# One attention layer of a decoder: a local and a global unit's values back to back, with copies, loads and the residual sum reordered around them

## The reference, cut to what matters

```python
x = x + attn(layernorm(x), ...)      # this layer is what the change touches
x = x + xattn(layernorm(x), ctx_1024, mask, ...)
x = x + ffn(layernorm(x), ...)       # 8 experts, top 2

def attn(x, ...):                    # x is (16, 256, 256): 16 batch rows, 256 tokens, width 256, 16 heads of 16
    x = x + pos_emb[:S]
    w = x.reshape(B, nW, 128, H, hd)                                  # windows of 128 tokens
    local = softmax(w @ w.T * scale) @ w                              # within a window, by head
    comp = conv(x, conv_w, stride 4) + conv_b                         # 64 compressed tokens a row
    gt = concatenate([comp, global_memory])                           # 128 global tokens
    glob = softmax(x @ gt.T * scale) @ gt                             # by head
    mix = sigmoid(concatenate([local, glob]) @ gate_w + gate_b)
    return (mix * local + (1 - mix) * glob) @ out_w + out_b
```

## Time and profile before

| what | value |
|---|---|
| three runs | 1135.87, 1140.89, 1145.44 us; median 1140.89 |
| profiled execution, its own time | 1146.37 us |
| its span, first to last instruction | 1144.5 us |
| granted TensorE clock over the span | 0.983 |
| PE busy | 1073.8 us (94%) |
| DVE, ACT, POOL busy | 675.0 (59%), 647.5 (57%), 543.9 us (48%) |
| self-attention | up to 438 us of the span |
| PE, DVE, ACT busy from 150 to 200 us | 48.11, 42.31, 30.87 of 50 us |

### The profile page before, as it was taken

How to read it: one execution, slowest core, us unless ns; L and a number is a source line. 1 busy time by engine, 2 the same in 40 slices (tenths; PEclk the granted TensorE clock), 3 DMA queues, 4 the chain that set the end, 5 groups by cost and what they waited for, 6 DMA issues and landing times.

```text
span 1144.5 us, 28496 instructions
## 1 busy us (share of the span) xinstructions
PE 1073.8 (94%) x11049; PEld 919.7 (80%) x11049; DVE 675.0 (59%) x1341; ACT 647.5 (57%) x870; POOL 543.9 (48%) x646
## 2 busy tenths in 40 slices
PE   7899999999999987999999998899999999999995
PEld 6777777787777765777777776799999999999995
DVE  4488888889878875788887888322424222222221
ACT  2466666656665653777776765444445444445441
POOL 6534455353653322443665553457654444444442
PEclk9899999999999997999999999999999999999999
DMA  8673653636436332566666567675433322233221
GB/s 214 168 179 109 148 152 88 180 107 160 128 83 183 77 100 48 149 189 174 145 150 150 144 159 205 181 174 56 42 52 49 52 47 48 47 51 51 48 42 24
DMA packets 174563, 130.23 MB, mean 114 GB/s; under 512 B 60810, under 2 KB 162927, under 8 KB 174432
## 3 DMA queue, kind: packets, MB, share of 16 engines
q1 hardware_dynamic: 155280, 106.79, 35.6%
q0 software_dynamic: 15840, 18.77, 11.7%
q10 hardware_dynamic: 3312, 2.85, 0.9%
HBM read 88.29 MB, written 40.08 MB: 112 GB/s over the span
## 4 chain that ended last, share of the span: by engine, by line
PE 48%; DMA 5%; DVE 3%; issue 2%; ACT 1%; another core or an unknown queue 1%; POOL 1%; SPq 1%; POOLq 0%; ACTq 0%
PE ps_scores L1861 22%; PE ps_out L1879 10%; PE ps_turn L1724 3%; DMA weights<-q_scr 3%; PE ps_misc L1756 2%; PE ps_out L1736 2%; PE ps_scores L1711 2%; PE ps_misc L1677 2%; DMA q_scr<-qp 2%; PE ps_turn L1840 1%; PE ps_misc L1744 1%; PE ps_scores L1704 1%; DVE xa_rowmax L2398 1%; DVE ps_scores L2395 1%; PE ps_turn L1766 1%
## 5 line engine op out<-in xcount | busy, mean ns | idle before, releaser
L1861 PEld LDWEIGHTS ps_scores<-xgT,weights 128*128 128x128 f32 x2272 | 263.8, 192 | 5.6 <-ACT xgT L2080 1.7
L1861 PE MATMUL ps_scores<-xgT,weights 128*128 128x128 f32 x2272 | 265.9, 275 | 1.4 <-ACT xgT L2080 1.1
L2367 DVE TENSOR_TENSOR gate<-ps_scores,silu 128x512 f32<-128x512 f32 x71 | 49.1, 692 | 243.7 <-ACT silu L2096 224.1
L915 ACT ACTIVATE weights<-ps_scores 128x1024 f32<-128x1024 f32 x128 | 126.9, 1023 | 81.1 <-PE ps_scores L608 65.7
L2096 ACT ACTIVATE silu<-ps_scores 128x512 f32<-128x512 f32 x71 | 42.4, 597 | 207.7 <-PE ps_scores L1861 199.1
L1879 PE MATMUL ps_out<-w2s,gate 128*128 x560 | 132.8, 380 | 0.8 <-DVE y L2373 0.8
L2089 ACT COPY weights<-weights 128x2048 f32 x68 | 129.9, 1910 | 0.5
L1879 PEld LDWEIGHTS ps_out<-w2s,gate 128*128 128x128 f32 x560 | 100.9, 190 | 12.3 <-issue 1.5
L1081 DVE TENSOR_REDUCE sa_rowmax<-ps_turn 128x8 bf16<-128x1024 f32 x64 | 77.7, 1215 | 34.4 <-PE ps_turn L585 34.4
L920 ACT CAST weights<-ps_scores 8x1024 bf16<-8x1024 f32 x64 | 64.3, 1004 | 54.2 <-PE ps_scores L599 54.2
L1555 POOL DMA_INDIRECT table<-entry,slot_i x64 | 64.7, 1011 | 47.1 <-PE ps_out L1736 24.8
(11 more groups left out here) (294 smaller groups left out, 2100.8 us busy)
## 6 DMA issues: line engine op xcount, KB each, us to landing
weights<-w_scr SPq DMA_DIRECT2D x60, 256.0 KB, 4.2
weights<-q_scr SPq DMA_DIRECT2D x96, 128.0 KB
ks<-w_scr SPq DMA_DIRECT2D x24, 256.0 KB, 3.8
weights<-k_scr SPq DMA_DIRECT2D x48, 120.0 KB
w_scr<-wp SPq DMA_DIRECT2D x7, 768.0 KB, 3.6
q_scr<-qp SPq DMA_DIRECT2D x14, 384.0 KB
weights<-in_w1T SPq DMA_DIRECT2D x10, 512.0 KB
weights<-in_w3T SPq DMA_DIRECT2D x10, 512.0 KB
```

Source lines behind the costliest of these rows:

```text
L915: act.activation(probs[s % 2][:], m.scores[s % 2][:], ACT.Exp, scale=SCALE).then_inc(exped, 1)
L1861: mm = pe.matmul(h_ps[r % 2][:, j, c, :], weights[:, j, k, c * P:(c + 1) * P], xgT[r % 2][:, k, :], start=(k == 0), stop=(k == DT - 1))
```

## The change: what it does, and the diff

Self-attention only. (1) On PE the two `values` calls of units 2k and 2k+1 follow each other, in four places of a row: behind `subtract_max(b+1, 0)`, behind `gate(b-1, 0)` (in odd rows behind `scores(b, 4)`), behind `gate(b-1, 1)` and behind `subtract_max(b, 6)` (in even rows behind `compress`). (2) Local probabilities get a second buffer, `m.first_probs`; an exponential of a local unit waits for the values four units back. `first_exponentials`, which wrote that buffer already, waits until it is read. (3) `turn_max` stands ahead of `scores` in each place, and ACT copies the turned maxima ahead of the context's copy. (4) `turn_c` writes `side[0]` (a half of `m.turn`) and no longer `m.misc`; `queries_scores(b, 3)` waits until ACT has read it. (5) On DVE `residual(b-2)` stands behind `maxima(b, 1)`, `apply_norm(b+3)` behind `maxima(b, 3)`, `mix_row(b-1)` behind `maxima(b, 7)`; in odd rows `maxima(b, 4)` stands ahead of `turn_out(b, 0, 0)`. (6) On SP the loads of a stack don't wait for each other, the store is a step of its own ahead of the last row's keys and values, and `load_g` stands ahead of `load_ctx`.

```diff
-    probs = m.wide
+    local_probs, global_probs = [m.wide[0], m.first_probs], m.wide[1]
+    probs = lambda U: global_probs if U % 2 else local_probs[U // 2 % 2]
...
-                if paced and (s > 2 or under_way):
-                    sp.wait_ge(loaded[s % 3], before + 16 * (s // 3))
+                if paced and under_way and s < 3:
+                    sp.wait_ge(loaded[s], before)
...
-        def stack_w(p):
+        def store_w(p):
             i = p % 2
             sp.wait_ge(w_split, 3 * R * (p + 1))
...
+        def stack_w(p):
+            i = p % 2
             sp.wait_ge(w_stored, 16 * p + 16)
...
+            store_w(p)
+            store_keys_values(R * p - 1)
             stack_w(p)
             store_g(p)
-            store_keys_values(R * p - 1)
+            load_g(p)
             load_ctx(R * p + 1)
-            load_g(p)
...
+            if old:
+                values(b - 1, UPR - 2)
+                values(b - 1, UPR - 1)
+            if not some:
+                first_scores()
+
+            if some:
+                turn_max(b, 1)
+                scores(b, 2)
             if more:
+                turn_c(b + 1, side[0])
+            if nxt or last and even:
                 if old:
                     pe.wait_ge(proj_read, b - 1)
...
-                turn_c(b + 1, m.misc)
-            if old:
-                values(b - 1, UPR - 1)
-            if some:
-                scores(b, 2)
-                turn_max(b, 1)
-            if nxt or last and even:
-                pe.wait_ge(cT_read, b + 2)
...
             if some:
-                values(b, 0)
                 keys_scores(b, 1)
             if some:
+                if more:
+                    pe.wait_ge(cT_read, b + 2)
                 queries_scores(b, 3)
                 subtract_max(b, 2)
...
                 gate(b - 1, 0)
-            if some:
+            if some and even:
+                values(b, 0)
                 values(b, 1)
             if some:
+                turn_max(b, 3)
                 scores(b, 4)
-                turn_max(b, 3)
+            if some and not even:
+                values(b, 0)
+                values(b, 1)
...
-                values(b, 2)
                 keys_scores(b, 3)
...
                 gate(b - 1, 1)
             if some:
+                values(b, 2)
                 values(b, 3)
             if some:
+                turn_max(b, 5)
                 scores(b, 6)
-                turn_max(b, 5)
...
-                values(b, 4)
                 keys_scores(b, 5)
...
                 if nxt and even:
                     compress(p + 1, 1)
+                values(b, 4)
                 values(b, 5)
+            if some:
+                turn_max(b, 7)
             if more:
                 scores(b + 1, 0)
-            if some:
-                turn_max(b, 7)
...
-                values(b, 6)
                 keys_scores(b, 7)
...
-            if U > 1:
+            if s % 2 and U > 1:
                 act.wait_ge(valued, U - 1)
-            act.activation(probs[s % 2][:], m.scores[s % 2][:], ACT.Exp, scale=SCALE).then_inc(exped, 1)
+            elif U > 3:
+                act.wait_ge(valued, U - 3)
+            act.activation(probs(U)[:], m.scores[s % 2][:], ACT.Exp, scale=SCALE).then_inc(exped, 1)
...
             act.wait_ge(m.shifted, 1)
+            act.wait_ge(valued, UPR * NB - 1)
...
                 exponentials(b, 0)
+            if some:
+                copy_max(b, 1)
             if more:
-                copy_cT(b + 1, m.misc)
-            if some:
-                copy_max(b, 1)
+                copy_cT(b + 1, side[0])
...
                 maxima(b, 1)
+            if b > 1:
+                residual(b - 2)
             if old:
                 turn_out(b - 1, 1, 1)
...
                 divide(b - 1, 1, 1)
+            if not some:
+                first_maxima()
+            if some:
+                maxima(b, 3)
             if ahead:
                 apply_norm(b + 3)
-            if not some:
-                first_maxima()
-            if some:
-                maxima(b, 3)
-                turn_out(b, 0, 0)
-                maxima(b, 4)
+            if some:
+                if even:
+                    turn_out(b, 0, 0)
+                    maxima(b, 4)
+                else:
+                    maxima(b, 4)
+                    turn_out(b, 0, 0)
                 divide(b, 0, 0)
                 maxima(b, 5)
                 turn_out(b, 0, 1)
                 maxima(b, 6)
+                maxima(b, 7)
             if old:
                 mix_row(b - 1)
             if some:
-                maxima(b, 7)
                 divide(b, 0, 1)
...
                 divide(b, 1, 0)
-            if old:
+            if not some:
                 residual(b - 1)
```

More of the change, by code:

```diff
@@ L637, in values @@
                     v = vg[i][:, f * HU + h, :] if kind else vl[i][:, n, f * HU + h, :]
-                    mm = pe.matmul(m.out[32 * j:32 * j + 32, 2 * kind + g, :], v, probs[s % 2][:, h, :], start=True,
+                    mm = pe.matmul(m.out[32 * j:32 * j + 32, 2 * kind + g, :], v, probs(U)[:, h, :], start=True,
                                    stop=True, tile_position=(0, 32 * j), skip_group_check=True)
@@ L739, in tensor_program @@
                     pe.wait_ge(gT_read, 1)
-                turn_c(b + 1, m.misc)
-            if old:
-                values(b - 1, UPR - 1)
-            if not some:
-                first_scores()
-            if some:
-                scores(b, 2)
-                turn_max(b, 1)
-            if nxt or last and even:
-                pe.wait_ge(cT_read, b + 2)
                 if even:
@@ L970, in scalar_program @@
                 exponentials(b, 0)
-            if more:
-                copy_cT(b + 1, m.misc)
             if some:
                 copy_max(b, 1)
+            if more:
+                copy_cT(b + 1, side[0])
             if (nxt or last) and even:
@@ L1173, in vector_program @@
                 divide(b - 1, 1, 1)
-            if ahead:
-                apply_norm(b + 3)
             if not some:
@@ L1180, in vector_program @@
                 maxima(b, 3)
-                turn_out(b, 0, 0)
-                maxima(b, 4)
+            if ahead:
+                apply_norm(b + 3)
+            if some:
[5 more added lines that the diff above has]
+                    turn_out(b, 0, 0)
                 divide(b, 0, 0)
```

## The result

| | before | after |
|---|---|---|
| median of the runs taken together (20 each) | 1139.1 us | 1145.93 us |
| after / before | | 1.0056, 95% interval 1.0039 to 1.0073 |
| profiled execution, its own time | 1146.37 us | 1149.72 us |
| its span; granted clock | 1144.5 us; 0.983 | 1147.9 us; 0.981 |
| end of row 15's q7 in the span | 420.74 us | 426.36 us |

The change makes the kernel slower by 0.56%, some 6.4 us. The prediction said 0.3 us faster. The last row of the table is the meter within a profile that the experiments use, row 15's q7: 5.62 us later. The first scores of the cross-attention, which the change does not touch, start 5.94 us later (438.30 us before, 444.24 us after).

What follows compares the result with a forecast made beforehand. PE was taken to bound the kernel on average, with DVE's chain binding from q7 to sub2. Six pairs at 49.3 against 48.57 us (+4.4) and the ends (-4.7) gave -0.3 us: 1140 us, range 1121 to 1153.

Steps and rivals of the forecast that it cites:

- C: Odd row's q7 to next row's sub2 (subtract_max(b, 2)): DVE's stretch, forecast 11.4 us from 10.35.
- D: Even row's sub2 to q7: PE's stretch, forecast 14.55 us from 14.22, merges -0.46, new waits 0.44 and 0.35.
- The merges: Second values call right behind the first on PE: saves 0.23 us a place, 1.84 us over a pair's eight.
- Rival 3: The wait between two values calls restores the 0.23 us, so merges save nothing: 1147 us; chance 0.07.
- The mixture: mix_row behind maxima(b, 7): the hole ahead stays and DVE's chain to sub2 grows by 1.33 us.
- A: Even row's q7 to next row's sub2: DVE's chain decides, forecast 11.6 us from 11.44.
- B: Odd row's sub2 to q7: forecast 11.75 us from 12.56, taking off 0.79 and 0.46, adding 0.44.
- rival 2: DVE and POOL collide in the longer chain, 0.5 us per mixture instruction: pair 51.3, kernel 1152 us; chance 0.15.
- The residual moves by one place within this chain and costs it nothing: DVE's chain from q7 to sub2: the residual's new place was priced at zero.
- The ends: Rows outside the six steady pairs: row 0 -2.3, row 14 -0.5, row 14 to 15 -1.4, row 15 -0.5, together -4.7 us.
- Rival 4: Unpaced loads near the start hold up out_w or the first stacks: +3 us, 1143 us; chance 0.05.
- Rival 1: DVE's hole ahead of maxima(b, 7) closes, so the mixture's place is free: pair 46.9, kernel 1126 us; chance 0.25.

Runs made afterwards that it cites:

- apply_even: Changed kernel with apply_norm(b+3) back ahead of maxima(b, 3) in even rows only; ratio to the kernel before 1.0063, pair 49.4 us.
- mix_ahead: Changed kernel with mix_row(b-1) back ahead of maxima(b, 7) on DVE; ratio to the kernel before 0.9952, pair 48.4 us.
- before_loads: Kernel before with only the changed kernel's SP program (loads and store); ratio to the kernel before 0.9988.
- tensor_part: Kernel before with only the change's PE and ACT part, DVE and SP programs as before; ratio to the kernel before 1.0061, pair 50.0 us.
- mix_residual: Changed kernel with mix_row(b-1) back ahead of maxima(b, 7) and the residual back at the row's end; ratio to the kernel before 0.9920.
- four_back: Changed kernel with mixture, residual and, in even rows with a next pair, apply_norm back; odd rows' values(b, 2), (b, 3) behind keys_values; ratio to before 0.9919.
- three_back: Changed kernel with mixture, residual and even-row apply_norm (with a next pair) back: ratio to before 0.9930; variants: old loads 0.9937, row 0's apply_norm left behind 0.9922.

## Why the prediction was wrong

**What bounds the kernel: right.** C was DVE's stretch and D was PE's. The two that the prediction thought would be DVE's are: sub2 waits 0.75 and 0.82 us for `sa_rowmax`, DVE is busy 11.11 of 11.68 and 11.12 of 11.53.

**The merges: right.** 1.01 us from the first call to the next group. The rule of the Trainium skill (page "TensorEngine Tiling (Array Packing)", section "Key Properties") that a change of tile within a mode needs no drain holds here: the second call starts 0.46 us after the first. Waits of weight loads ahead of `values` on their own engine fell from 64 (16.9 us) to 25 (7.7 us). Rival 3, that the merges save nothing, is out.

**The new waits: right.** 0.48 us (0.44 predicted) for ACT's copy. The position sum cost 0.36 in D (0.35 predicted), which apply_even took away.

**The mixture: right in C, and larger than it looks in A.** Predicted 11.6 and 11.4, measured 11.68 and 11.53. But mix_ahead shows that only 0.15 us of A is the mixture's own; the rest of it would have been waits and the residual.

**The sum of the stretches was mis-sized, 49.3 for 49.8.** B is 0.22 over: the prediction had taken all of its 0.79 us of waits and drains off; without the new wait it is 11.49 us where 11.31 was counted. C is 0.13 over: the mixture's second instruction, where rival 2 put the hit, took 1.16 for 0.69 us. The prediction's own 11.07 without a hit and these 0.47 make 11.54, and 11.53 was measured. A is 0.08 and D 0.07 over. Over six pairs 0.5 us is 3.0 us of the error. Rival 2 thus came true by half: one hit in C, and none in A, where the mixture takes 0.68 and 0.69 us.

**The size of a hit** can be read from the rows, and is not the 0.5 us that rival 2 took for each. In C, POOL's instruction had 0.61 us left when DVE's started, and DVE's grew by 0.47. In the 360 multiplications of `divide` and instructions of the mixture that started between 62 and 410 us of the fourteen profiles while a POOL instruction had over 0.2 us left, DVE's grew, over the 0.42 and 0.69 us that they take alone, by what was left less 0.13 to 0.15 us. What was left was 0.2 to 1.1 us, and there is no exception. But for these 0.14 us the trace agrees with the Trainium skill (page "SBUF — State Buffer", section "Who interferes with whom"), both on which instruction suffers and on its waiting for the whole of the other.

**"The residual moves by one place within this chain and costs it nothing": wrong.** 0.24 us a pair, by two experiments. The sum lies in front of `maxima(b+1, 2)` in both orders, but the old one let it run before DVE's wait for q1 in `maxima(b+1, 1)`, and the new one puts it behind that wait (0.36 us in mix_ahead; 0.16 in the changed kernel, where it explains only a part of the 0.24). In a chain without gaps, which the prediction assumed, the place would be free. The term was put at zero and is a third of the 0.73 that was forecast.

**The ends: wrong, and the largest step.** The prediction gave them -4.7 us; they gave -1.7. Either this error or that of the pairs would have turned the sign of a forecast of -0.3. Measured by the same cuts:

- Row 0, -2.3 predicted; row 1 had no term. Counted from `gate_b`, the way to row 2's sub2 fell from 50.67 us (39.15 to 89.82) to 50.05 (40.77 to 90.82), -0.62. Row 0 gains 1.3 in it up to its q7 and loses 0.2 behind, and row 1's B gains 0.6. Then C from row 1 to 2 loses 1.06 (10.47 to 11.53): the longer DVE chain begins with row 1's q7. In row 0, 1.4 us of PE's idle time were to go; from q1 to q1 it fell from 2.86 to 2.15, and why no more went is not shown. The regime has seven stretches C, and the prediction counted six. In the profiles as they are, `out_w` came 1.62 us later after the change. From its issue to `gate_b` the kernels with the new loads took 5.6 to 7.5 us (nine profiles) and those with the old ones 6.2 to 6.6 (five), so this is mostly the execution; a small effect of the loads is not excluded.
- Row 14 to 15, -1.4 predicted. 14.08 to 12.20 looks like more. But before_loads, which has the order of before on PE and DVE, took 12.45 us there: 1.6 of the 14.08 us was a half-clock stretch (clock 0.88 in the earlier trace rows) of that one profile. The change is worth 0.25. What the prediction left out is again the mixture. It had reckoned with PE's wait for ACT alone, and that wait is there, 1.16 us. But DVE's chain with the mixture in it is now the longer way, 11.76 us busy of 12.20. mix_ahead, with the mixture back in its hole, takes 10.97 us there, 1.48 less than before_loads, which is the predicted gain.
- Row 14 was right (-0.51, predicted -0.5).
- Row 15, -0.5 predicted. Up to q7 it gained 0.67 (11.16 to 10.49), but 0.3 of it is lost again behind q7, where the projection waits 1.08 us for the mixture. From sub2 to the first scores of the cross-attention it is -0.34; mix_ahead has -0.92 there.

The stretch from row 14 to 15 in the changed kernel: the mixture on DVE and what POOL did beside it, then PE's waits.

```profile
405.71 1.62 DVE L1128 SCALAR_TENSOR_TENSOR diffT<-diffT,weights 128x512 f32<-128x512 f32 x1
405.64 1.16 POOL L423 TENSOR_TENSOR rest<-wT,wp 128x512 f32<-128x512 f32 x1 [4.70 <-ACT wp L880]
```

```profile
407.49 1.96 PE L681 MATMUL ps_misc<-out_w,diffT 128*128 128x256 f32 x8 [0.25 <-DVE diffT L1128]
...
412.54 0.26 PE L604 MATMUL ps_scores<-neg_ident,sa_rowmax 128*104 128x128 bf16 x1 [0.57 <-DVE sa_rowmax L1092]
```

**The failed steps in one place.** The mixture's cost of 1.3 us was right in C. Where the chain with it binds was wrong: it also binds after row 1, from row 14 to 15 and in row 15, where the prediction had priced none of it or too little. With half of row 0's idle time, which stayed, the ends so came to -1.7 us for -4.7. Beside that the sum of a pair was 0.5 us short.

**The account.** Without the two accidents (`out_w`'s +1.6 and the half-clock stretch's -1.6) the part up to the cross-attention is some 5.9 us longer: 7.38 for six pairs, 0.3 for row 13's end, -0.62, -0.51, -0.25, -0.34. The forecast was 4.4 - 4.7 = -0.3. Of the 6.3 us between, 3.3 are pairs, 1.7 rows 0 and 1, 1.1 row 14 to 15, and 0.2 row 15. The time behind row 15's q7 varied more than all this, from 712 to 724 us over the fourteen profiles, though nearly all of it is the same work. So the profiled executions differ by 3.35 us where the runs differ by 6.4.

**"Issued in 6 us": wrong, without a consequence.** SP takes 12.3 to 13.2 us for the twelve. Six alone take 3.8, and the kernel still waits ahead of three key loads, which the prediction, and the description of the change ahead of it, had left out. That the loads cost nothing was right, twice (0.9988 and 0.9937 to 0.9930). Rival 4, a flood at the start, is not seen in these ratios.

**What was not asked.** The prediction priced `maxima(b, 4)` ahead of `turn_out(b, 0, 0)` and `apply_norm` behind `maxima(b, 3)` by their harm alone. In odd rows they are what the tensor part needs: 1.1 us a pair each. It never asked what the PE change would be without them. The change is thus three things: a new order on PE and ACT that by itself costs 1.4 us a pair (tensor_part, 50.0), two DVE steps in odd rows that bring 2.2 and make it a gain (47.8), and three more moves on DVE (the mixture, the residual, `apply_norm` in even rows) that cost 2.0 and turn it into a loss (49.8).

Rival 1, the closing of the hole, did not happen (1.96 and 1.70 us stand in front of `maxima(b, 7)`); and the changed kernels that have the mixture in the hole again (mix_ahead, mix_residual, four_back and the three_back ones) stay above its numbers, a pair of 46.9 and 1126 us: their pairs take 47.8 to 48.4 us and their ratios of 0.992 to 0.995 make some 1130 to 1134.

## What to carry to other kernels

A step with slack belongs in a hole of its engine, in front of the instruction that the hole waits for, and not behind it: the mixture behind `maxima(b, 7)` left 1.96 us empty and put 1.3 us on the path. When a merge frees one engine, go through the other engines' queues for what must now come earlier, as each such order was worth 1.1 us a pair here, against 1.84 for the merges (the prediction's sum of eight places). Count where a regime begins and ends by asking in which row the new bound first holds and in which it last does; here the two stretches that were missed, after row 1 and from row 14 to 15, cost 1.1 and 1.2 us. And a stretch with a clock under 1 is compared only with the same stretch of another execution.

## What the runs showed of the hardware

- The clock fell to its half level behind a wait of PE in one row and not behind the same wait in another row of the same execution: 0.88 us of idle time was followed by 3.49 us for one projection (clock 0.51) and by 1.96 for another.
- SP issues these loads 0.65 us apart where no wait stands between them, six in 3.8 us.
- An instruction of DVE with two inputs in SBUF that starts beside a running POOL instruction grows by what is left of that one, less 0.13 to 0.15 us: 0.47 for 0.61 left, 0.94 for 1.08, in all 360 cases of the fourteen profiles.
- A second `values` call behind the first goes through at the pace of the rounds, 0.46 us, although its own semaphore wait stands between them.
- The time behind row 15's q7 differed by up to 12 us between executions of nearly the same work.
